# Idle matmuls ahead of 57 chosen items of TensorE, and a newly searched order of all queues, in a fused recurrence, attention and mixture-of-experts kernel

## The chip, the cores and the metric

One Trainium2 chip, one of its cores. The time is that of one execution on the device in microseconds, from its start to its end, as the median of several runs. TensorE multiplies, VectorE (DVE) and ScalarE (ACT) do the elementwise work, GpSimd (POOL) does the additions of the recurrence and some masks, and SyncE (SP) issues every DMA, one after the other in one written order.

## The reference

The input x has the shape (4, 1024, 256). Two layers follow one another, each as x + layernorm(layer(layernorm(x))).

```python
# layer 1: a gated recurrence over the 1024 steps of time
px = x @ W_state.T + b_state
g  = sigmoid(x @ W_gate.T + b_gate)
state = tanh(px[t] + state); out[t] = g[t] * state
# layer 2: attention, then a mixture of four experts
q, k = rms(heads(h @ wq.T)), rms(heads(h @ wk.T)); v = heads(h @ wv.T)     # 16 heads of 16
x = x + softmax(causal(q @ k.T / 4)) @ v @ wo.T                            # first 64 columns set to 0
w = top 2 of 4 of softmax(xf @ gate_w.T), renormalised
o0 = gelu(xf @ e0_up.T) @ e0_down.T
o1 = silu(xf @ e1_w1.T) * (xf @ e1_w2.T) @ e1_down.T
o2 = gelu(gelu(gelu(xf @ e2_l1.T) @ e2_l2.T) @ e2_l3.T) @ e2_l4.T
o3 = gelu(gelu(xf @ e3_down.T) @ e3_up.T) @ e3_out.T
x = x + sum_e w[e] * o_e                                                   # first 64 columns set to 0
```

## The kernel before, in words

The work is cut into items. An item is a key such as `("qk", 3, 0)` and stands for a handful of instructions of one engine, or for one transfer of SP. There are 1648 items of TensorE, 909 transfers, 1100 items of DVE, 840 of ACT and 98 of POOL, and beside these the 1024 steps of the recurrence, each a pair of `sadd` (POOL, L1959) and `stanh` (ACT, L1185).

First comes a stage of 8 tiles of 128 moments of time for all four batches: load x (`xin`), layernorm on DVE (`hst`, `hsc`), transpose on TensorE (`htr`), copy (`hcp`), the two products with W_state and W_gate (`hpx0`, `hpx1`), and the store of what is needed later (`hsv`). It ends with `hpx0, 7`. Beside it and after it 19 pieces of the expert weights are loaded (`wl`), split by DVE into a rounded part that stays and a remainder (`wsh`, `wsp`, L1593 and L1599), and the remainders are written back to memory (`wst`, L1041). The load of a piece waits for the split of the fourth one before it, since they share four buffers.

Then come 16 units u of 256 rows (`NU`), each one a chain: load of the gate values (`gl`), gating with the state of the recurrence on DVE (`pgate`), transposes (`ptr`), load of x (`xl`), two layernorms on DVE (`pln`, `pu`), `qh`, `qtr`, the products for q, k and v (`qk`, `vm`), their normalisation on DVE (`qrs`, `kh`, `qq`), transposes (`kt`, `qt`), tiles of scores for the row maxima (`mxm` on TensorE, `mxr` on DVE), `mtr`, `mta`, a small transfer `mtd`, then scores, exponentials and weighted values (`sc`, `ex`, `av`), the output projection (`wo`), the router (`gm`, `ga`, `gb`), and the experts: `up`, `gel`, `dn` with weights that SP loads anew for each unit (`wr`). The last step of a unit is `fin` and its store `ost`. Units overlap: the experts of one unit run beside the attention of the next ones.

What sets the order. `Plan.sequence` merges all items into one list. `PLACES` gives, kind by kind, the place of each item in that list, and `STEPS` tells how many items stand between a step of the recurrence and the next. Each engine executes its items in this order, with nothing reordered at run time, and each item first waits on the semaphores of what it needs. `Plan.run` goes once through the list with estimated durations, and from that decides which of the eight banks of PSUM and which buffer each item gets; a bank or buffer that was held before adds a wait (`turn`, `freed`). `ISSUE`, `RATE` and `FLIGHT` are its estimates for transfers. The estimated times are used for nothing else.

On TensorE an item waits first for its bank (`freed(key, "P2")`, `freed(key, "P1")`), then for its operands. `mm` at L1299 is a matmul, `tr` at L1302 a transpose, L1383 the transposes of `kt` and `qt`. A plain f32 product stands in the profile as two matmul records, one of rounded operands or a transpose as one. The pool `MB` (two buffers, taken by `mxm`, given back by `mxr`) exists in the plan; the code of `mxm` waits for its bank, but not for `MB`.

Of the kernel before, what the change touches and what calls it, by code (L numbers as in the profile page):

```python
# [42 lines left out]
BANKS = {"P2": 2, "P1": 1}  # L43
# [3 lines left out]
HOP = 0.04  # L47
# [4 lines left out]
ISSUE, RATE, FLIGHT = 0.47, 300.0, 1.7  # L52
# [4 lines left out]
    "wl": (9, 6, 10, 4, 5, 8, 53, 209, 99, 227, 222, 229, 3, 198, 208, 206, 199, 221, 223, 219, 214, 256, 242, 255, 226,  # L57
        267, 250, 286, 282, 291, 264, 290),
    "cbx": (24,),
    "cqk": (237,),  # L60
    "wsp": (101, 132, 98, 129, 211, 218, 216, 213, 240, 236, 241, 225, 263, 245, 279, 244, 284, 262, 289, 378, 303, 327,
        329),
    "wsh": (210, 217, 215, 212, 234, 233, 239, 224, 261, 243, 278, 235, 281, 259, 288, 283, 297, 280, 302),
    "wst": (220, 231, 228, 309, 252, 266, 257, 232, 319, 268, 354, 477, 287, 265, 320, 471, 475, 433, 470),
    "wdd": (308, 598, 137, 269),
    "xin": (0, 7, 26, 54, 55, 96, 102, 150),
    "hst": (11, 21, 28, 69, 71, 118, 128, 179),
    "hsc": (13, 16, 12, 14, 25, 37, 41, 22, 39, 40, 38, 42, 75, 73, 70, 76, 74, 77, 78, 72, 121, 120, 123, 119, 134, 130,
        131, 133, 182, 181, 183, 180),
    "htr": (15, 17, 18, 19, 43, 45, 46, 47, 44, 48, 50, 51, 81, 82, 83, 84, 85, 86, 87, 88, 124, 125, 126, 135, 140, 141,  # L70
        142, 143, 185, 186, 189, 190),
    "hcp": (20, 49, 52, 89, 110, 144, 147, 191),
# [3 lines left out]
    "hgt": (30, 31, 32, 33, 34, 35, 36, 64, 65, 66, 67, 91, 92, 93, 59, 60, 62, 68, 106, 107, 108, 104, 105, 109, 112, 113,  # L76
        114, 115, 136, 152, 153, 155, 157, 161, 163, 159, 160, 162, 165, 166, 170, 171, 156, 167, 168, 169, 172, 173, 174,
        193, 195, 196, 201, 202, 203, 204),
    "hout1": (61, 94, 116, 117, 164, 176, 175, 205),
    "hsv": (95, 97, 138, 139, 149, 178, 151, 194, 187, 188, 207, 230),  # L80
    "ident": (1,),
    "consts": (2,),
    "pxl": (530, 1523),
    "gl": (100, 251, 478, 352, 805, 960, 1026, 1141, 1557, 1748, 1809, 1910, 2710, 2271, 2970, 3072),
    "xl": (247, 258, 536, 473, 954, 968, 1074, 1219, 1750, 1802, 1872, 2242, 2942, 2415, 3020, 3427),
    "pgate": (238, 253, 497, 452, 930, 964, 1043, 1184, 1702, 1781, 1828, 1934, 2737, 2323, 3010, 3195),
    "ptr": (246, 254, 506, 459, 933, 966, 1049, 1207, 1716, 1787, 1830, 2218, 2934, 2396, 3016, 3409),
    "pcp": (248, 271, 580, 487, 940, 972, 1062, 1209, 1722, 1793, 1836, 2239, 2952, 2406, 3032, 3412),
    "pln": (249, 272, 589, 488, 963, 1000, 1081, 1247, 1752, 1819, 1876, 2286, 2979, 2416, 3034, 3439),
# [3 lines left out]
    "qtr": (273, 307, 614, 511, 985, 1016, 1109, 1293, 1769, 1859, 2130, 2332, 3013, 2528, 3125, 3498),  # L93
    "qhT": (274, 312, 617, 513, 992, 1024, 1114, 1303, 1772, 1863, 2132, 2335, 3023, 2548, 3170, 3501),
    "qhl": (275, 314, 618, 518, 994, 1047, 1126, 1322, 1783, 1940, 2139, 2351, 3028, 2552, 3174, 3508),
    "qk": (276, 292, 317, 331, 621, 635, 522, 541, 995, 1006, 1050, 1085, 1201, 1225, 1326, 1381, 1815, 1831, 1987, 2020,
        2148, 2211, 2370, 2472, 3033, 3080, 2614, 2756, 3307, 3338, 3521, 3694),
    "qkc": (277, 294, 326, 333, 622, 638, 523, 543, 999, 1010, 1057, 1088, 1208, 1230, 1332, 1386, 1818, 1837, 2012, 2021,
        2158, 2220, 2374, 2477, 3035, 3083, 2617, 2766, 3314, 3342, 3526, 3697),
    "qred": (285, 295, 330, 335, 630, 656, 529, 556, 1003, 1012, 1065, 1091, 1214, 1248, 1365, 1393, 1826, 1841, 2013, 2057,  # L100
# [3 lines left out]
    "vst": (310, 392, 778, 566, 1078, 1143, 1370, 1530, 1873, 2243, 2315, 2720, 3208, 2909, 3509, 3855),  # L104
    "qrs": (296, 336, 659, 557, 1015, 1093, 1253, 1394, 1850, 2058, 2232, 2483, 3093, 2783, 3359, 3722),
# [6 lines left out]
    "kst": (311, 321, 355, 393, 674, 693, 569, 647, 1048, 1098, 1190, 1223, 1278, 1313, 1428, 1518, 1875, 1911, 2080, 2118,  # L112
# [7 lines left out]
    "ktm": (322, 323, 324, 353, 405, 406, 430, 431, 705, 706, 735, 736, 804, 821, 859, 860, 1102, 1104, 1107, 1142, 1224,  # L120
# [4 lines left out]
    "mxm": (339, 340, 344, 345, 359, 360, 363, 364, 367, 369, 370, 373, 375, 376, 383, 384, 409, 410, 414, 416, 422, 423,  # L125
# [259 lines left out]
)  # L385


class Plan:

# [1606 lines left out]
```

## Time and profile before

| | us |
|---|---|
| median of 3 runs | 1581.17 |
| lowest, highest | 1580.75, 1584.56 |
| the profiled execution | 1590.62 |
| its span, first to last instruction | 1588.9 |
| TensorE busy in it | 1401.2 (88%) |
| mean granted TensorE clock | 0.933 |

The profile is of one execution. Busy times are the time in which an engine had an instruction in it. The granted clock is 1.0 where TensorE was allowed its full 2.4 GHz and 0.5 where it got 1.2 GHz; the page shows it in 40 slices, and a stretch of the trace can be asked for its mean. An idle time in square brackets is the engine's own just before the row, with what ended it.

### The profile page before, as it was taken

What the parts mean: (1) busy time and instruction counts of PE and PEld (TensorE: products, weight loads), DVE (VectorE), ACT (ScalarE), POOL (GpSimd) and SP (SyncE); (2) the same over time, 40 slices, a digit from 0 to 9 for tenths busy, and PEclk for the clock granted to TensorE, in tenths of its full rate; (3) what the DMA queues carried; (4) which work ended last, traced back from release to release, by engine and by line L of the source; (5) the groups of instructions that cost most, each with busy time, mean ns of one, the idle gap of its engine ahead of it and who ended that gap; (6) DMA issues with size and microseconds to landing.
All of it is one profiled execution on the core that took longest, in us unless ns stands there. A gap on an engine that the chain in (4) does not pass through costs nothing.

```text
span 1588.9 us, 33612 instructions
## 1 busy us (share of the span) xinstructions
PE 1401.2 (88%) x12320; PEld 1111.7 (70%) x12320; DVE 1098.1 (69%) x2916; ACT 884.0 (56%) x2042; POOL 310.1 (20%) x1146
## 2 busy tenths in 40 slices
PE   6924679888999799997999999999999899999997
PEld 3413568877788468875878668875788557885797
DVE  6856466655688876668888777778799648783334
ACT  2544546654665585576555773437631686337942
POOL 3333223332233332223233110001000010001000
PEclk9966569997999799998999999998999999999999
DMA  3464455674467457664547646585667566676544
GB/s 113 141 212 146 138 173 151 181 205 144 149 181 220 142 145 215 192 187 128 194 144 219 201 139 199 149 247 155 185 187 228 154 215 192 200 221 189 158 144 134
DMA packets 244275, 278.53 MB, mean 175 GB/s; under 512 B 37136, under 2 KB 167696, under 8 KB 243856
## 3 DMA queue, kind: packets, MB, share of 16 engines
q1 hardware_dynamic: 244112, 276.39, 58.0%
q8 instruction: 99, 1.62, 0.4%
q14 instruction: 64, 0.52, 0.1%
HBM read 234.18 MB, written 43.45 MB: 175 GB/s over the span
## 4 chain that ended last, share of the span: by engine, by line
PE 59%; DMA 12%; DVE 10%; ACT 9%; issue 5%; SPq 3%; POOL 3%; ACTq 0%; DVEq 0%
PE PS L1299 54%; DMA KT<-ktd 5%; ACT work L1253 3%; PE PS L1302 3%; POOL AD L1959 2%; DMA WB<-wlo_e_l 2%; ACT PX L1185 2%; PE PS L1383 1%; DVE mx L1758 1%; DMA WB<-wdn_e_down 1%; DVE st L1576 1%; DMA work<-in_L_ffn_e_l 1%; DMA UU<-in_L_attn_x 1%; POOL work L1966 1%; SPq L1051 1%
## 5 line engine op out<-in xcount | busy, mean ns | idle before, releaser
L1185 ACT ACTIVATE PX<-AD 128x8 f32<-128x8 f32 x1023 | 219.7, 215 | 253.8 <-POOL AD L1959 252.6
L1959 POOL TENSOR_TENSOR AD<-PX 128x8 f32<-128x8 f32 x1023 | 242.4, 237 | 580.4 <-ACT PX L1185 567.5
L1253 ACT ACTIVATE work<-PS 128x1024 f32<-128x1024 f32 (+1 forms) x312 | 286.2, 959 | 77.7 <-PE PS L1299 76.7
L1758 DVE TENSOR_REDUCE mx<-PS 128x2 f32<-128x1024 f32 (+3 forms) x256 | 256.7, 1020 | 64.8 <-PE PS L1299 64.3
L1299 PE MATMUL PS<-work,vlx 128*32 128x256 f32 (+2 forms) x2816 | 242.5, 388 | 19.0 <-ACT work L1253 5.4
L1278 ACT ACTIVATE work<-PS 128x512 f32<-128x512 f32 x176 | 102.5, 593 | 177.4 <-PE PS L1299 176.7
L1299 PE MATMUL PS<-EP,u_e_l 128*128 128x256 f32 x1024 | 195.0, 285 | 7.0 <-DMA WB<-wlo_e_l 4.8
L1299 PE MATMUL PS<-WB,work 128*128 128x192 f32 x1024 | 186.4, 337 | 7.5 <-DMA WB<-wdn_e_down 4.7
L1966 POOL TENSOR_SCALAR_AFFINE_SELECT work<-work 128x512 f32<-128x512 f32 x96 | 63.0, 667 | 625.5 <-ACT work L1253 625.4
L1299 PEld LDWEIGHTS PS<-WB,work 128*128 128x128 f32 x1024 | 170.7, 195 | 12.8 <-issue 6.2
L1299 PE MATMUL PS<-EP,WB 128*128 128x256 f32 x640 | 179.3, 280 | 0.0
L1299 PEld LDWEIGHTS PS<-EP,u_e_l 128*128 128x128 f32 x1024 | 161.1, 189 | 10.6 <-issue 4.9
L1299 PEld LDWEIGHTS PS<-work,vlx 128*32 128x32 f32 (+1 forms) x2816 | 90.6, 118 | 109.9 <-issue 52.2
L1299 PE MATMUL PS<-KT,QT 64*128 64x512 f32 (+3 forms) x768 | 146.6, 427 | 22.4 <-DMA KT<-ktd 9.9
L1299 PE MATMUL PS<-XF,WB 128*128 128x256 f32 x576 | 163.9, 285 | 0.0
L1299 PE MATMUL PS<-QT,KT 64*128 64x256 f32 (+1 forms) x1344 | 143.9, 320 | 20.5 <-DMA KT<-ktd 7.9
L1299 PEld LDWEIGHTS PS<-QT,KT 64*128 64x128 f32 x1344 | 102.1, 199 | 83.4 <-issue 57.3
L1758 DVE TENSOR_REDUCE mxb<-PS 128x2 f32<-128x256 f32 (+3 forms) x128 | 104.8, 819 | 31.2 <-PE PS L1299 30.7
L1299 PEld LDWEIGHTS PS<-EP,WB 128*128 128x128 f32 x640 | 121.2, 189 | 0.1
L1299 PEld LDWEIGHTS PS<-KT,QT 64*128 64x128 f32 x768 | 72.0, 197 | 62.8 <-issue 29.9
L1299 PEld LDWEIGHTS PS<-XF,WB 128*128 128x128 f32 x576 | 111.5, 194 | 0.1
L1299 PE MATMUL PS<-XF,u_e_w 128*128 128x256 f32 x512 | 101.6, 287 | 1.7 <-DMA WB<-wlo_e_w 1.7
(170 smaller groups left out, 2244.8 us busy)
## 6 DMA issues: line engine op xcount, KB each, us to landing
KT<-ktd SPq DMA_DIRECT2D x112, 512.0 KB, 5.0
WB<-wlo_e_l SPq DMA_DIRECT2D x160, 256.0 KB, 4.1
ktd<-KTs SPq DMA_DIRECT2D x128, 128.0 KB, 2.6
WB<-wlo_e_up SPq DMA_DIRECT2D x64, 256.0 KB, 3.5
WB<-wlo_e_w SPq DMA_DIRECT2D x64, 256.0 KB, 3.7
WB<-wdn_e_down SPq DMA_DIRECT2D x64, 192.0 KB, 3.0
KT<-ktd SPq DMA_DIRECT2D x48, 256.0 KB, 3.7
KT<-ktd SPq DMA_DIRECT2D x32, 384.0 KB, 4.2
```

The lines of the kernel that those rows point to most:

```text
L1051: eng.dma_start(plain(WB[place[key, "W"]][:, :, 0:src.shape[2]]), src).then_inc(of(*key), 16)
L1185: eng.activation(cur, AD[n % 2], ACT.Tanh).then_inc(of(*key), 1)
L1253: eng.activation(pt[:, :, :, q0:L], two("sc", *a).rearrange("p a (l q) -> p a l q", l=2)[:, :, :, q0:L], ACT.Exp).then_inc(of(*key), 1)
L1278: eng.activation(half_of(hidden(u, name), h), one("up", u, name, h), ACT.Gelu).then_inc(of(*key), 1)
L1299: return eng.matmul(o, l, r, start=start, stop=stop, skip_group_check=skip)
L1302: return eng.transpose(o, i, ident)
L1383: ins = eng.transpose(ps[:, p // 4, 128 * (p % 4):128 * (p % 4) + 128].bitcast(F32R), QKP[:, 2 * p:2 * p + 2, :].rearrange("p h r -> p (h ...
L1576: step(eng.bn_stats(s_[:, i, :], src[:, i, :]))
L1758: eng.tensor_reduce(o, two("mxm", *a)[:, :, 0:w], AX, ALU.max, negate=True).then_inc(of(*key), 1)
L1959: eng.tensor_tensor(AD[n % 2], PX[c % 2][:, :, :, t], PX[(n - 1) // L % 2][:, :, :, (n - 1) % L], ALU.add).then_inc(of(*key), 1)
L1966: eng.affine_select(out=p, in_=p, compare_op=ALU.is_ge, fill=0.0, base=0, pattern=[[0, 2], [0, 2], [1, 128]], channel_multiplier=-1).then_ ...
```

## The change

Three things are changed.

- A table `WARM` names 57 items of TensorE and a number for each, 190 in all. Ahead of such an item, after the wait for its bank and before the wait for its operands, TensorE does that many f32 products of the identity with itself, 128 x 128 by 128 columns, into the bank that the item holds and is about to overwrite. Their results are used by nobody.
- `PLACES` and `STEPS` are new tables throughout. Of the 1648 items of TensorE 709 change their place in TensorE's own order, 136 of them by three places or more and 8 by ten or more (at most 16). Of SP's 909 transfers 766 move, 370 by three or more and 85 by ten or more (at most 83). Of DVE's 1100 items 755 move, 203 by three or more. Of ACT's 840 items 405 move, 74 by three or more. On POOL 4 items move by one.
- The estimates of the plan are changed: issue and flight times by kind of transfer in place of 0.47 and 1.7 for all, and the idle products are in its account of TensorE's time and of its clock. They act on the kernel through the choice of banks and buffers alone.

The core of the diff, without the number tables:

```diff
-ISSUE, RATE, FLIGHT = 0.47, 300.0, 1.7
+RATE, IDLE = 300.0, 0.222
+ISSUE = {"kst": 0.66, "vst": 0.54, "mtd": 0.73, "gl": 0.64, "kts": 0.62, "vl": 0.62, "wr": 0.6, "x1l": 0.62}
+FLIGHT = {"gl": 2.55, "hsv": 1.55, "kst": 0.55, "ktm": 2.35, "kts": 2.55, "ost": 2.05, "vl": 2.25, "vst": 3.55, "wr": 2.1, "wl": 2.25,
+          "wst": 1.65, "x1l": 2.25, "x1st": 1.95, "xin": 1.95, "xl": 1.75, "pxl": 3.5, "wdd": 2.15, "mtd": 1.35}
...
+WARM = {
+    ("aot", 0): 1, ("aot", 2): 1, ("av", 0, 3, 0): 4, ("av", 1, 0, 0): 6, ("av", 1, 1, 0): 1, ("av", 10, 1, 0): 3,
+        ("av", 2, 1, 0): 2, ("av", 6, 3, 0): 1, ("dn", 11, "e2_l4"): 5, ("dn", 15, "e3_out"): 4, ("dn", 2, "e1_down"): 7,
+        ("dn", 6, "e3_out"): 3, ("gm", 2): 9, ("gm", 7): 1, ("hpx0", 0): 3, ("kt", 0, 0): 7, ("kt", 0, 1): 2,
+        ("kt", 1, 0): 5, ("kt", 4, 0): 3, ("kt", 6, 0): 6, ("mtr", 3): 4, ("mxm", 0, 2): 11, ("mxm", 0, 6): 6,
+        ("mxm", 1, 10): 2, ("mxm", 1, 13): 1, ("mxm", 1, 5): 1, ("mxm", 13, 23): 2, ("mxm", 2, 10): 2, ("mxm", 3, 9): 5,
+        ("mxm", 5, 1): 3, ("mxm", 5, 11): 1, ("mxm", 5, 4): 3, ("ptr", 0): 7, ("ptr", 1): 8, ("ptr", 4): 1, ("qk", 0, 0): 8,
+        ("qk", 0, 1): 2, ("qk", 1, 0): 2, ("qk", 15, 0): 1, ("qk", 8, 1): 4, ("qt", 2, 0): 3, ("qt", 8, 0): 2,
+        ("qtr", 0): 2, ("qtr", 2): 2, ("qtr", 3): 1, ("qtr", 5): 1, ("sc", 0, 1, 0): 1, ("sc", 1, 0, 0): 1,
+        ("sc", 1, 2, 0): 12, ("sc", 12, 0, 0): 1, ("sc", 9, 3, 0): 1, ("up", 0, "e0_up", 0): 4, ("up", 15, "e2_l2", 0): 2,
+        ("up", 8, "e2_l3", 0): 1, ("vm", 2): 1, ("wo", 0): 2, ("wo", 1): 5
+}
...
+                if key in WARM:
+                    bank = PS[:, place[key, "P2" if (key, "P2") in place else "P1"], :]
+                    pe.wait_ge(*done("ident"))
+                    for _ in range(WARM[key]):
+                        mm(bank[:, 0:128], ident, ident, True, True, True)
```

In `Plan.run` the idle products are run from the moment at which the bank is free in the plan, `IDLE` us each at the full clock and twice that at half of it, and the item starts after them. The plan's account of the clock counts its stretches from the start of the plan, before and after the change.

In SP's order the transfers that the prediction speaks of stand as follows. Before, `hsv, 7, 1` (the last store of gate values) stood at place 45 of SP's list, behind thirteen loads of weights (`wl`), among them `e2_l2, 1, 1`, and behind two stores of remainders (`wst`). Now it stands at place 42, behind the loads of `e1_w2` and `e2_l1` and behind `wst, e0_up, 0, 0`, and ahead of all loads of `e2_l2`, of `wl, n1` and of `wst, e1_w1, 0, 0`. `wl, qn`, which stood just ahead of it, is at place 29. `wl, wo` has gone from place 34 to place 101. Between `xl, 0` and `gl, 1` stood one load; now a store and a load stand there.

## Rows read from the trace of the kernel before

**Rows 1.** The page: busy time of each engine; TensorE and clock by slices; the chain.

```profile
PE 1401.2 (88%) x12320; PEld 1111.7 (70%) x12320; DVE 1098.1 (69%) x2916; ACT 884.0 (56%) x2042; POOL 310.1 (20%) x1146
...
PEclk9966569997999799998999999998999999999999
...
PE 59%; DMA 12%; DVE 10%; ACT 9%; issue 5%; SPq 3%; POOL 3%; ACTq 0%; DVEq 0%
```

**Rows 2.** Busy time by stages: stretch, length, each engine, granted clock, DMA share, GB/s.

```profile
85.00:160.00 75.00, 22.34 (x95) 16.60 (x94) 49.01 (x139) 31.16 (x127) 27.09 (x105) 0.64 0.61 186
160.00:230.00 70.00, 49.95 (x462) 38.01 (x460) 37.18 (x119) 32.23 (x103) 17.49 (x78) 0.59 0.54 162
...
230.00:1588.90 1358.90, 1261.77 (x11580) 1024.89 (x11580) 952.02 (x2469) 784.11 (x1655) 236.46 (x836) 0.96 0.60 179
```

**Rows 3.** The same view, of the seventeen half-clock stretches between 230 and 1580 us.

```profile
417.22:424.05 6.83, 6.83 (x73) 4.96 (x72) 5.86 (x23) 5.24 (x9) 0.61 (x3) 0.50 0.37 115
...
sum 92.17, PE 84.58 PEld 66.05 DVE 62.82 ACT 43.88 POOL 21.62; mean PE 4.98 PEld 3.89 DVE 3.70 ACT 2.58 POOL 1.27
```

**Rows 4.** The same view, of the half-clock stretches between 90 and 230 us.

```profile
164.64:209.01 44.37, 35.48 (x351) 27.98 (x352) 23.05 (x61) 18.46 (x62) 12.01 (x52) 0.50 0.48 137
...
sum 112.63, PE 59.25 PEld 45.53 DVE 69.89 ACT 47.11 POOL 32.96; mean PE 14.81 PEld 11.38 DVE 17.47 ACT 11.78 POOL 8.24
```

**Rows 5.** TensorE's timeline, 85 to 170 us: start, length, instruction, [idle before <- what ended it].

```profile
106.22 1.09 PE L1302 MATMUL PS<-ident,G 128*128 128x128 f32 x4 [18.56 <-DMA gd<-work]
...
114.88 1.12 PE L1302 MATMUL PS<-ident,G 128*128 128x128 f32 x4 [7.57 <-DVE G L1674]
...
126.16 1.19 PE L1299 MATMUL PS<-wqkv,hT 128*128 128x512 f32 x2 [3.85 <-DVE hT L1615]
...
140.49 1.23 PE L1383 MATMUL PS<-identr,QKP 128*128 128x128 f32 x8 [7.87 <-DVE QKP L1749]
...
168.63 1.23 PE L1383 MATMUL PS<-identr,QKP 128*128 128x128 f32 x8 [2.06 <-DVE QKP L1749]
```

**Rows 6.** SP's timeline around the last store of gate values.

```profile
94.33 0.47 SPq L1041 DMA_DIRECT2D wlo_e_up<-WB  x1
...
99.50 0.52 SPq L1062 DMA_DIRECT2D gd<-work  x1
```

**Rows 7.** TensorE's timeline: two rows at half clock, two at full clock.

```profile
227.35 1.11 PE L1302 MATMUL PS<-ident,G 128*128 128x128 f32 x4
228.25 1.06 PE L1302 MATMUL PS<-ident,HA 128*128 128x128 f32 x4
...
610.98 2.87 PE L1299 MATMUL PS<-WB,work 128*128 128x192 f32 x16
613.68 0.60 PE L1302 MATMUL PS<-ident,HA 128*128 128x128 f32 x4
```

**Rows 8.** TensorE's waits after 230 us: for whom, us in total, times, longest.

```profile
PE PS L1299 <- DMA KT<-ktd: 14.1, 14, 3.4
PE PS L1299 <- ACT work L1253: 12.2, 20, 1.9
...
PE PS L1299 <- DMA WB<-wlo_e_l: 5.8, 5, 2.9
```

**Rows 9.** TensorE's timeline: first and last of 34 `WARM` items after 230 us.

```profile
230.19 0.63 PE L1302 MATMUL PS<-ident,HA 128*128 128x128 f32 x4 [0.87 <-DVE HA L1718]
...
1578.37 1.86 PE L1299 MATMUL PS<-WB,work 128*128 128x192 f32 x10 [0.78 <-ACT work L1278]
```

**Rows 10.** TensorE's timeline: the longest wait for a transfer after 160 us.

```profile
224.31 1.12 PE L1299 MATMUL PS<-QT,KT 64*128 64x128 f32 x8 [3.65 <-DMA KT<-ktd]
```

**Rows 11.** DVE's gating of unit 4, and two steps of the recurrence on ACT behind it.

```profile
402.17 0.69 DVE L1670 SCALAR_TENSOR_TENSOR G<-G,PX 128x512 f32<-128x512 f32 x1 [0.50 <-ACT PX L1185]
...
403.48 0.21 ACT L1185 ACTIVATE PX<-AD 128x8 f32<-128x8 f32 x1 [0.31 <-POOL AD L1959]
404.01 0.22 ACT L1185 ACTIVATE PX<-AD 128x8 f32<-128x8 f32 x1 [0.31 <-POOL AD L1959]
```

More of the change, by code:

```diff
@@ L56 @@
 PLACES = {
[L57 to L64, printed above, removed]
@@ new lines @@
+    "cbx": (27,),
+    "cqk": (228,),
+    "wsp": (227, 135, 75, 102, 210, 204, 207, 209, 236, 229, 250, 237, 262, 239, 285, 280, 278, 261, 296, 356, 338, 312,
+        409),
+    "wsh": (208, 203, 205, 206, 233, 226, 232, 225, 252, 235, 282, 277, 276, 260, 295, 326, 284, 279, 357),
+    "wst": (223, 266, 238, 242, 473, 258, 289, 246, 263, 257, 406, 471, 351, 286, 403, 394, 431, 321, 434),
+    "wdd": (319, 255, 106, 7),
+    "xin": (0, 4, 24, 54, 57, 100, 108, 150),
+    "hst": (8, 18, 44, 55, 69, 103, 130, 167),
@@ L125 @@
-    "mxm": (339, 340, 344, 345, 359, 360, 363, 364, 367, 369, 370, 373, 375, 376, 383, 384, 409, 410, 414, 416, 422, 423,
[19 rows of a table removed]
-    "mxr": (341, 342, 348, 347, 361, 362, 365, 366, 368, 371, 372, 374, 379, 377, 387, 386, 413, 412, 418, 419, 424, 425,
[19 rows of a table removed]
-    "mtr": (388, 463, 769, 893, 1216, 1351, 1588, 1717, 2128, 2371, 2772, 2995, 3387, 3575, 3982, 4181),
-    "mta": (389, 467, 771, 894, 1217, 1363, 1607, 1762, 2129, 2372, 2782, 3012, 3396, 3597, 3984, 4191),
-    "mtd": (396, 476, 781, 911, 1222, 1368, 1649, 1805, 2133, 2402, 2794, 3021, 3426, 3598, 4038, 4253),
[4 rows of a table removed]
@@ new lines @@
+    "gl": (194, 245, 474, 265, 584, 954, 1031, 1163, 1591, 1759, 1807, 1879, 2821, 2240, 2973, 3216),
+    "xl": (241, 259, 535, 493, 952, 997, 1042, 1218, 1707, 1806, 1877, 2268, 2971, 2414, 3017, 3411),
+    "pgate": (230, 251, 483, 455, 932, 963, 1032, 1171, 1693, 1766, 1844, 1992, 2866, 2301, 3008, 3221),
+    "ptr": (231, 254, 505, 468, 933, 979, 1033, 1196, 1697, 1783, 1856, 2222, 2940, 2397, 3012, 3409),
+    "pcp": (240, 269, 528, 491, 936, 983, 1034, 1202, 1698, 1811, 1858, 2230, 2957, 2400, 3026, 3431),
@@ new lines @@
+    "pln": (243, 270, 587, 499, 955, 999, 1078, 1226, 1736, 1813, 1883, 2287, 2978, 2440, 3031, 3440),
[3 rows of a table added]
+    "qtr": (271, 303, 613, 511, 981, 1015, 1115, 1283, 1770, 1870, 2114, 2326, 3011, 2519, 3124, 3496),
+    "qhT": (272, 310, 616, 513, 982, 1025, 1116, 1292, 1779, 1889, 2125, 2337, 3020, 2540, 3160, 3505),
+    "qhl": (273, 311, 621, 519, 991, 1052, 1124, 1319, 1782, 1937, 2131, 2338, 3025, 2557, 3167, 3509),
+    "qk": (274, 291, 315, 329, 624, 632, 522, 541, 993, 1007, 1059, 1084, 1199, 1215, 1322, 1380, 1791, 1827, 1981, 2019,
+        2152, 2215, 2369, 2472, 3029, 3079, 2609, 2758, 3307, 3338, 3520, 3695),
@@ new lines @@
+    "kst": (305, 318, 354, 391, 671, 704, 592, 642, 1049, 1094, 1181, 1222, 1277, 1359, 1426, 1524, 1882, 1911, 2079, 2120,
[7 rows of a table added]
+    "ktm": (322, 323, 350, 353, 404, 405, 432, 433, 707, 730, 739, 740, 788, 828, 860, 861, 1099, 1100, 1161, 1180, 1223,
[4 rows of a table added]
+    "mxm": (336, 337, 343, 344, 358, 360, 362, 364, 366, 367, 369, 375, 377, 379, 381, 382, 411, 413, 414, 416, 422, 423,
[19 rows of a table added]
+    "mxr": (339, 340, 348, 347, 359, 361, 363, 365, 368, 370, 371, 376, 378, 380, 384, 383, 412, 415, 419, 421, 425, 426,
[19 rows of a table added]
+    "mtr": (385, 476, 784, 898, 1211, 1347, 1580, 1721, 2129, 2383, 2769, 2993, 3388, 3575, 3991, 4176),
@@ L431, in run, with clock, stream, enter @@
         got, end, busy, mode, wire = {}, {}, dict.fromkeys(self.order, 0.0), dict.fromkeys(self.order), 0.0
-        streamed, window, slow = defaultdict(float), 0, False
+        streamed, window, slow, after = defaultdict(float), 0, False, None
+        def clock(t):
+            nonlocal window, slow
+            while (window + 1) * WINDOW <= t:
+                slow = t > FRESH and streamed[window] / WINDOW < (HIGH if slow else LOW)
+                window += 1
+            return 2.0 if slow else 1.0
+        def stream(t, us):
+            t1 = t + us
+            while t < t1:
+                w = int(t / WINDOW + 1e-9)
+                streamed[w] += min(t1, (w + 1) * WINDOW) - t
+                t = min(t1, (w + 1) * WINDOW)
+        def enter(m, gap):
+            if m != mode["pe"]:
+                mode["pe"] = m
+                return ENTER[m] + max(0.0, (LEAVE.get(after, 0.095) if after else 0.0) - gap)
+            return ENTER[m] if gap > 0.05 else 0.0
         for k in self.sequence():
             e, us, take, m, kb = self.items[k]
-            t = max([busy[e]] + [end[a] if (a, k) in self.queue else self.over[a] + HOP for a in self.after[k]])
+            bank, t = 0.0, max([busy[e]] + [end[a] if (a, k) in self.queue else self.over[a] + HOP for a in self.after[k]])
             for p in take:
@@ L454, in run @@
                 t = max(t, a)
+                if p in BANKS:
+                    bank = a
                 self.place[k, p] = got[k, p][0]
@@ L461, in run @@
             if e == "pe":
-                while (window + 1) * WINDOW <= t:
-                    slow = t > FRESH and streamed[window] / WINDOW < (HIGH if slow else LOW)
-                    window += 1
-                us *= 2.0 if slow else 1.0
-                t0, t1 = t, t + us
-                while t0 < t1:
-                    w = int(t0 / WINDOW + 1e-9)
-                    streamed[w] += min(t1, (w + 1) * WINDOW) - t0
-                    t0 = min(t1, (w + 1) * WINDOW)
-                gap = t - busy[e]
-                if m != mode[e]:
-                    us += ENTER[m] + max(0.0, (LEAVE.get(self.order[e][-1][0], 0.095) if self.order[e] else 0.0) - gap)
-                elif gap > 0.05:
-                    us += ENTER[m]
-                mode[e] = m
+                if k in WARM:
+                    t1 = max(busy[e], bank)
+                    for i in range(WARM[k]):
+                        d = IDLE * clock(t1)
+                        if i == 0:
+                            d += enter("128", t1 - busy[e])
+                        stream(t1, d)
+                        t1 += d
+                    busy[e], after = t1, "idle"
+                    t = max(t, t1)
+                us *= clock(t)
+                stream(t, us)
+                us += enter(m, t - busy[e])
+                after = k[0]
             elif m and m != mode[e]:
@@ L482, in run @@
                 wire = max(wire, t + us) + kb / RATE
-                over = wire + FLIGHT
+                over = wire + FLIGHT[k[0]]
             self.order[e].append(k)
@@ L542, in dma @@
     def dma(key, kb, *after, n=1, **more):
-        add("sp", key, ISSUE * n, *after, kb=float(kb), **more)
+        add("sp", key, ISSUE.get(key[0], 0.52) * n, *after, kb=float(kb), **more)
     for i, w in enumerate(("x0", "bs", "bg", "x1", "q", "k", "v", "wo", "gw", "n1", "n2", "qn", "kn")):
```

120 lines of the change are left out of this document (54 added, 66 removed), and 490 rows, old and new, of tables (PLACES, STEPS).

## The prediction

> **What bounds the kernel now.** I read the page first. TensorE is busy 1401.2 of 1588.9 us, no other engine more than 1098.1, and the chain that ended last is TensorE for 59% [rows 1]. The slices of the clock add what the busy time hides: a dip to 0.5 and 0.6 early on, and single slices of 0.7 later [rows 1]. Then I cut the span into stages. From 230 us on TensorE is busy 1261.77 of 1358.90 us, so it is the bound there and only 97 us are idle; from 85 to 160 us it is busy 22 of 75 us, from 160 to 230 us 50 of 70 us [rows 2]. The second stretch is bound by a chain: the loads and splits of the weights, and unit 0 going from engine to engine.
>
> Last I asked for the stretches at half clock, 1.2 in place of 2.4 GHz. Between 230 and 1580 us there are seventeen, 92.17 us long with TensorE busy 84.58 of them [rows 3]. Work that takes 84.6 us at half clock takes some 42 us at full clock: 42 us is all that the clock has to give there. Between 90 and 230 us there are four, 112.63 us with 59.25 us busy; in the longest of them, 164.64 to 209.01 us, it is 35.48 of 44.37 us [rows 4]. In the other three TensorE mostly waits, and a faster clock shortens only what the chain passes through.
>
> **The price of an idle product.** A plain product of 192 columns at full clock takes (613.68 - 610.98) / 16 = 0.169 us a record, which for two records of 128 columns makes 2 x 0.169 x 128/192 = 0.225 us. At half clock four records of 128 columns take 228.25 - 227.35 = 0.90 us, so a product of two records takes 0.45 us [rows 7]. The 190 products are 43 us of TensorE at full clock and 86 at half. Whether they cost anything depends on the wait that they stand in. I laid the places of `WARM` on the trace of before. 95 products lie before 230 us and 95 behind it.
>
> **Part 1, SP's order at 85 to 110 us.** The first transposes of unit 0 wait 18.56 us, until 106 us, for the store of gate values [rows 5]. That store is issued at 99.50 us [rows 6]: ahead of it stand loads and stores that wait for DVE's splits. In the new order it stands right behind `wst, e0_up, 0, 0`, which before was issued at 94.33 us [rows 6], and the loads of `e2_l2` that block are behind it. That is 99.5 - 95.0 = 4.5 us. The next step of unit 0, `xl`, is issued behind `ptr`, and the transposes of unit 1, at 114.88 us [rows 5], depend on `gl, 1`, which is moved along. Bounds: 0, if the gating on DVE or the landing is late instead, and 8. I take **-4.5**. Moved past the store are the loads of `e2_l2`, which now come later; what hides this is that their weights are first used after 250 us.
>
> **Part 2, the clock up to 160 us.** Ahead of `ptr`, `ptr`, `qtr`, `qk` and `kt` of units 0 and 1 stand 7, 8, 2, 8 and 7 products, at most 3.6 us at half clock; four of the five waits they stand in are 18.56, 7.57, 3.85 and 7.87 us long [rows 5]. They are free. They come at the start of the wait, so of a long wait most stays idle, and I don't expect the level to hold through 8 or 18 us. Where the wait is as long as the products (`qk, 0, 0`: 8 x 0.45 = 3.6 of 3.85 us) the level can be up for what follows. The chain passes through `qk` and `kt` for about 4 us at half clock; half of it is **-2**, bounds 0 and -4.
>
> **Part 3, 160 to 230 us.** `mxm, 0, 2` gets 11 products, `kt, 1, 0` five and `mxm, 0, 6` six. Before, `mxm, 0, 2` followed its predecessor without a gap; the plan sees a wait there for `MB`, which the code doesn't have. The next real wait is the 2.06 us at `kt, 1, 0` [rows 5]. The 22 products take 5 us at full clock and 10 at half, less 2.06: 3 to 8 us late, beside DVE's work on the keys in part; queued behind them are the tiles of scores that DVE reduces, and behind these `mtr` and the transfer of the maxima. I take +3. If the clock is up for the 35.48 busy us [rows 4], that gives up to 17.7; ACT's exponentials and DVE pace part of it, so I take -8. The 18 products at `sc, 1, 2, 0` and `av, 1, 0, 0` are 4.1 us at full clock beside the 3.65 us for the transfer of keys that stands two items on [rows 10]: nothing. Together **-5**, bounds +8 and -15.
>
> **Part 4, the clock after 230 us.** Of the seventeen stretches twelve have items of `WARM` in them or in the 8 us ahead, with 61.6 of the 84.58 busy us; five, such as 417.22 to 424.05 us, have none [rows 3]. The twelve could give 30.8 us. The level falls after thin stretches, and the order of hundreds of items around has changed, so new dips will come; I take half, -15. The 95 products cost 21.4 us. Of the 34 items 18 stood behind a gap of 0.15 us or more, the first 0.87 us, the last 0.78 us [rows 9]; gap by gap these cover 9.8 us. Of the other 11.6 us I take half as cost, +6, since the new order can have put a wait where the trace has none. Together **-9**, bounds +12 (no clock) and -25.
>
> **Part 5, the order after 230 us.** The waits for keys and for the experts' remainders sum to 19.9 us [rows 8]. Better issue and flight times place loads earlier, -3. A TensorE that is faster in places runs into ACT and POOL; there are 12.2 us of waits for the exponentials already [rows 8]: +3. Together **0**, bounds -12 and +10.
>
> **The sum.** -4.5 - 2 - 5 - 9 + 0 = -20.5 us. The profiled execution took 1590.62 us, 9.4 more than the median of 1581.17; as the terms are differences, I set them against the median: 1581.2 - 20.5 = **1560.7 us**.
>
> **The rivals.**
> Products without their clock. They were placed for a clock that the plan counts from its own start. If the level in a run changes at other moments, the dips stay and the products remain. The trace speaks for it in part: the five stretches without any product nearby show that the plan didn't expect them. Price: parts 2 and the -8 and -15 fall away, the products cost 3 + 6 and up to the full 3 + 11.6, against -4.5: +4.5 to +10, so about 1588 us, slower. It decides where less than 9 us of the clock's gain come. [...] Chance 0.11. The Trainium skill ("TensorE: Matmul & The Clock Gate", Part 1) says that the gate's count runs free and isn't reset at a kernel's start, so that the same kernel meets it at a different phase each time; no single trace can show that, and by it this rival is the natural one.
>
> The gain goes into other waits. TensorE is relieved, and DVE, ACT and transfers are late next. At unit 4 there is a place for this: its gating ran right behind the 512th step of the recurrence, at 402.17 us [rows 11], 4 us ahead of its transposes, so that a lead of more than that before 400 us is lost unless the recurrence comes earlier too. For that speaks that undisturbed steps follow at 0.53 us (404.01 - 403.48, [rows 11]), while 512 steps by 402 us are 0.79 each: they are held up by ACT's other work, which would move along. If half of parts 3 and 4 is lost this way: -4.5 - 2 - 7 = 1568 us, between 1564 and 1577. Chance 0.22.
>
> Nothing is left. Part 1 is hidden by DVE, and clock and products cancel: 1580 us. Chance 0.09.
>
> All of it holds. The twelve stretches give 25 us and the long one at 165 us gives 12: 1541 us. Chance 0.08.
>
> **How the numbers follow.** The forecast, 1550 to 1573 us, has 0.50. Within 0.3%, about what a measurement of this kernel can tell from no change, is 1576.4 to 1585.9. Faster: 0.50 + 0.08 + 0.20 of the 0.22 = 0.78; same: 0.09 + 0.02 = 0.11; slower 0.11. For 8 in 10 the range reaches from 1544 to 1582.
>
> **What would show it.** Part 1: the store of gate values issued at about 95 us and the first transposes of unit 0 at 101 to 102 us. Part 2: `qk, 0, 1` at full clock. Part 3: `kt, 1, 0` late by 1 to 5 us, and the scores of unit 0 nevertheless 3 to 9 us earlier, with the clock at 1.0 up to 209 us. Part 4: half-clock stretches after 230 us of 50 to 60 us in place of 92, and a mean clock of 0.95 or more. Part 5: TensorE's waits for keys and remainders not above 20 us. I am wrong if the half-clock time after 230 us is above 80 us, if TensorE's other waits grow by more than 10 us, or if unit 0 starts no earlier.

## The result, and the profile after

The changed kernel takes 1536.83 us (1536.3 to 1538.04, 4 runs) against 1582.87 us (1580.75 to 1584.91, 4 runs): ratio 0.9696, 95% interval 0.9666 to 0.9726. That is 46 us faster. I had forecast 20 us and a range down to 1544 us. The sign was right, the size was not. The two profiled executions lie 54 us apart (1590.62 and 1536.93 us): that of the kernel before was 8 us above its median, so differences between the two traces are too large by about that much.

The page of the changed kernel: busy times, TensorE's clock in 40 slices, the chain that ended last.

```profile
span 1535.2 us, 34359 instructions
...
PE 1417.4 (92%) x12700; PEld 1138.7 (74%) x12700; DVE 1096.4 (71%) x2916; ACT 877.5 (57%) x2038; POOL 311.9 (20%) x1146
...
PEclk9977689999999899999999999999999999999999
...
PE 69%; DVE 12%; ACT 7%; DMA 4%; issue 4%; POOL 2%; SPq 2%; ACTq 0%; DVEq 0%
```

Beside [rows 1] TensorE is busy 16 us longer and the span is 54 us shorter. The 380 new matmul records are the 190 products. The main change is in the chain: transfers held 12% of it, now 4%. The late slices of 0.7 are gone from the clock; the early dip is shorter, but it is there.

The same stages as in [rows 2], cut where unit 0 has come as far (224 us), and the sum of the half-clock stretches after that, for [rows 3]:

```profile
85.00:156.00 71.00, 32.84 (x174) 29.23 (x173) 48.58 (x139) 33.49 (x130) 26.73 (x98) 0.71 0.64 195
156.00:224.00 68.00, 58.08 (x562) 47.60 (x562) 36.77 (x112) 27.48 (x94) 16.50 (x76) 0.72 0.52 151
224.00:1535.20 1311.20, 1258.24 (x11774) 1027.90 (x11771) 951.88 (x2477) 780.05 (x1656) 239.84 (x839) 0.99 0.62 186
...
sum 30.71, PE 29.18 PEld 19.69 DVE 19.79 ACT 15.40 POOL 7.44; mean PE 4.17 PEld 2.81 DVE 2.83 ACT 2.20 POOL 1.06
```

The gain lies in the third stage. Its length went from 1358.9 to 1311.2 us, its idle time from 97 to 53 us, though 95 products fill part of it, and its half-clock time from 92.2 us in seventeen stretches to 30.7 in seven.

TensorE's longest waits there, for [rows 8]:

```profile
PE PS L1337 <- ACT work L1291: 7.4, 19, 1.4
PE PS L1337 <- POOL work L2009: 5.5, 9, 1.5
PE PS L1426 <- DVE QKP L1792: 4.7, 6, 1.4
PE PS L1337 <- DVE mx L1801: 3.7, 9, 0.9
PE PS L1337 <- DMA KT<-ktd: 3.1, 2, 2.0
```

The waits for keys were 14.1 us and are 3.1. The waits for the experts' remainders `wlo_e_l`, 5.8 us, and for `wdn_e_down` are no longer among them; the latter stood in the kernel before as

```profile
PE PS L1299 <- DMA WB<-wdn_e_down: 4.7, 4, 2.2
```

The waits for ACT's exponentials became shorter too, not longer: 12.2 us before, 7.4 now.

Where the lead arises can be read by laying the items of the two traces on one another. The last expert product of a unit comes earlier by 6 us in unit 1, 22 in unit 3, 34 in unit 5, 54 in unit 8, and by 54 in unit 15: it grows from 350 to 1010 us and not at all afterwards.

### The profile page after: what moved, and what is told of

Its sections match the earlier page's. It is cut to its first block, busy times and chain, and to the rows that moved or that the text cites. A ratio compares the mean times of both kernels' runs of the same rounds, so it can differ in the third digit from the quotient of the medians.

```text
span 1535.2 us, 34359 instructions
## 1 busy us (share of the span) xinstructions
PE 1417.4 (92%) x12700; PEld 1138.7 (74%) x12700; DVE 1096.4 (71%) x2916; ACT 877.5 (57%) x2038; POOL 311.9 (20%) x1146
## 4 chain that ended last, share of the span: by engine, by line
PE 69%; DVE 12%; ACT 7%; DMA 4%; issue 4%; POOL 2%; SPq 2%; ACTq 0%; DVEq 0%
PE PS L1337 64%; PE PS L1340 3%; ACT work L1291 3%; PE PS L1426 2%; POOL AD L2002 1%; DVE mx L1801 1%; ACT PX L1223 1%; DMA KT<-ktd 1%; DMA vlx<-vd 1%; DVE st L1619 1%; DMA WB<-wlo_e_w 1%; DVE mxb L1801 1%; POOL work L2009 1%; ACT work L1316 1%; DVE rst L1606 0%
## 5 line engine op out<-in xcount | busy, mean ns | idle before, releaser
L1337 PE MATMUL PS<-work,vlx 128*32 128x256 f32 (+2 forms) x2816 | 236.2, 378 | 14.6 <-POOL work L2009 5.5
L1337 PE MATMUL PS<-WB,work 128*128 128x192 f32 x1024 | 182.2, 332 | 1.0 <-ACT work L1316 0.6
L1337 PEld LDWEIGHTS PS<-WB,work 128*128 128x128 f32 x1024 | 166.5, 191 | 5.2 <-issue 1.8
L1337 PE MATMUL PS<-XF,WB 128*128 128x256 f32 x576 | 160.8, 279 | 0.0
L1337 PE MATMUL PS<-KT,QT 64*128 64x512 f32 (+3 forms) x768 | 144.0, 419 | 10.5 <-DVE mx L1801 4.3
L1337 PEld LDWEIGHTS PS<-QT,KT 64*128 64x128 f32 x1344 | 97.2, 191 | 69.2 <-issue 47.4
L1337 PE MATMUL PS<-QT,KT 64*128 64x256 f32 (+1 forms) x1344 | 137.3, 311 | 8.8 <-DMA KT<-ktd 3.1
L1337 PEld LDWEIGHTS PS<-XF,WB 128*128 128x128 f32 x576 | 108.3, 188 | 0.2
```

The lines of the kernel that those rows point to most:

```text
L1337: return eng.matmul(o, l, r, start=start, stop=stop, skip_group_check=skip)
```

## The experiments

For each trace I give four numbers of one stretch, from the transposes of unit 0 in its expert part (`xtr, 0`) to the last expert product: its length, TensorE's idle time in it, how much of that idle time a transfer ended, and the excess of the clock, which is half of TensorE's busy time in half-clock stretches. They come from single executions, and executions of one kernel scatter: 64 runs of the kernel before, on four chips, took 1574.0 to 1595.0 us. The times and ratios come from all runs of a kernel; a ratio is to the kernel before on the same chip, whose median was 1582.9 to 1586.9 us.

| kernel | median us | ratio to before (95%) | length | idle | by transfers | half-clock us (stretches) | excess |
|---|---|---|---|---|---|---|---|
| before | 1582.9 | | 1350.1 | 90.1 | 31.1 | 93.4 (18) | 42.8 |
| changed | 1536.8 | 0.9696 (0.9666-0.9726) | 1300.7 | 45.3 | 7.8 | 30.7 (7) | 14.6 |
| changed, again (e9) | 1539.5 | 0.9700 (0.9666-0.9734) | 1298.0 | 44.0 | 6.9 | 27.3 (5) | 12.2 |
| new order, no products (e1) | 1540.8 | 0.9699 (0.9665-0.9733) | 1309.0 | 66.5 | 14.3 | 57.4 (9) | 24.7 |
| the same again (e10) | 1543.5 | 0.9711 (0.9676-0.9746) | 1310.7 | 65.8 | 11.4 | 61.0 (10) | 26.7 |
| old order, products (e2) | 1592.6 | 1.0029 (1.0000-1.0058) | 1346.1 | 76.1 | 19.7 | 58.0 (13) | 27.1 |
| changed, late products only (e3) | 1540.9 | 0.9707 (0.9677-0.9738) | 1303.3 | 46.1 | 10.8 | 37.0 (7) | 16.8 |
| transposes for products (e4) | 1537.1 | 0.9692 (0.9648-0.9736) | 1298.9 | 48.2 | 10.5 | 23.9 (4) | 9.8 |
| SP's order old, rest new (e5) | 1623.3 | 1.0238 (1.0174-1.0303) | 1363.7 | 96.1 | 35.6 | 109.8 (20) | 48.2 |
| SP's order new, rest old (e6) | 1672.7 | 1.0557 (1.0493-1.0621) | 1407.7 | 117.2 | 31.2 | 161.4 (24) | 71.8 |
| old order, new banks (e7) | 1596.8 | 1.0081 (1.0046-1.0115) | 1359.8 | 90.6 | 24.2 | 106.7 (18) | 48.1 |
| TensorE's order old, rest new (e8) | 1732.2 | 1.0933 (1.0871-1.0996) | 1485.5 | 169.8 | 22.6 | 209.5 (38) | 90.9 |
| fitted products (e11) | 1535.5 | 0.9668 (0.9635-0.9701) | 1296.8 | 36.1 | 3.0 | 17.1 (3) | 7.9 |
| first part new (e12) | 1571.7 | 0.9891 (0.9854-0.9928) | 1337.7 | 84.0 | 22.7 | 75.4 (13) | 32.9 |
| second part new (e13) | 1573.6 | 0.9934 (0.9911-0.9957) | 1341.4 | 85.0 | 21.1 | 85.3 (12) | 37.6 |
| old order, 14 transfers ahead (e14) | 1580.6 | 0.9971 (0.9951-0.9991) | 1335.8 | 80.7 | 15.5 | 81.9 (13) | 36.8 |
| old order, one store ahead (e15) | 1586.8 | 1.0019 (0.9998-1.0040) | 1346.0 | 95.2 | 29.5 | 73.3 (12) | 30.5 |

### Order or products?

Run e1 leaves the products out of the changed kernel, e2 puts them into the one before.

```diff
-                if key in WARM:
+                if key in ():
```

> The changed kernel with its new order and its choice of banks and buffers, but without the 190 idle products on TensorE. Theory A (the new order gives the larger part, because TensorE waits less for transfers; the products give the rest through the clock): 1548 to 1558 us, half-clock time after 230 us between 55 and 90 us, TensorE's waits for transfers after 230 us at most 15 us, as in the changed kernel. Theory B (the products give nearly all of it through the clock): 1570 us or more. Theory C (the products do nothing that the order would not do alone): 1535 to 1540 us.

> The kernel before, in its old order, with the same 190 products ahead of the same 57 items. Theory A: between 1568 and 1585 us: the clock gives back 10 to 20 us and the products that stand in no wait cost 5 to 15; the waits for transfers stay at about 30 us. Theory B: 1545 to 1560 us. The rival of the prediction (products without their clock): 1585 to 1592 us.

The new order alone gives 45 us (0.9699). The products alone, in the old order, give nothing and rather cost 5 us (1.0029). For the time of e1 theory C was nearest (1535 to 1540 us), and A, with an order worth 28 to 38 us, was 7 us off; A's two other marks held (57.4 us at half clock, 14.3 us of waits for transfers). For e2 no theory held: by the time the rival, 1585 to 1592 us, was nearest.

The order's gain adds up in the table: idle time 90.1 to 66.5 (-23.6), clock 42.8 to 24.7 (-18.1), together -41.7 of a length that fell by 41.1. So the order, which says nothing of clocks, gave back about as much of the clock as the products: 18.1 us here and 16.1 in the second trace of this kernel (e10), against 15.7 for the products in the old order (e2) and 10.1 and 14.5 in the new one. TensorE's waits in the order-only kernel, e1, after unit 0:

```profile
PE PS L1337 <- ACT work L1291: 8.1, 16, 1.2
PE PS L1426 <- DVE QKP L1792: 8.0, 8, 1.4
PE PS L1337 <- DVE mx L1801: 6.0, 12, 1.2
...
PE PS L1337 <- DMA WB<-wdn_e_down: 3.5, 2, 2.0
...
PE PS L1337 <- DMA KT<-ktd: 2.9, 5, 0.9
```

The keys and most of the remainders have left the list here already, with no product in the kernel.

In e2 the products do give back clock, 42.8 to 27.1, and fill waits, 90.1 to 76.1; that is 29.7 us. But 95 products take at least 21.4 us, the stretch is only 4.0 us shorter in all, and before it unit 0 comes 5.8 us later (234.1 in place of 228.3 us). In all: nothing.

The ten runs of e2 show something that one trace can't: how much clock comes back differs from run to run, and the time with it. The mean granted clock was 0.946 in the slowest (1600.2 us) and 0.964 in the fastest (1580.8 us). Each of the ten is above all 64 runs of the kernel before, 0.925 to 0.941.

### The products, within the new order

> The changed kernel itself once more, to stand beside the order-only kernel on the same chip. 1535 to 1542 us.

> The order-only kernel (changed kernel without its 190 products) once more, on the same chip as the changed one. The two medians of different calls were 4 us apart. If the products are worth something in the new order: 3 to 6 us above the changed kernel. If they are worth nothing: within 2 us.

On one chip the changed kernel took 1539.5 us (1530.5 to 1546.8) and the order-only one 1543.5 us (1533.3 to 1546.9). That is 4 us, as between e1 and the first result, but the runs overlap widely; the products are worth about 4 us, and these runs don't rule out that they are worth nothing. What they do to the clock is beyond doubt: its mean is 0.956 to 0.965 in the ten runs with products (the first four and e9) and 0.940 to 0.949 in the ten without (e1 and e10). The traces show how: from e10 to e9 the clock gives 14.5 us, the idle time falls by 21.8, and the products take 21.4; the stretch is 12.7 us shorter, in the other pair 8.3. The profiled run of e9 was its fastest and that of e10 nearly its slowest, so 12.7 is too much. The dips that stay are mostly at the same places: the changed kernel's at 507.5, 524.5, 558.7 and 698.6 us are found in e9, some 6 us ahead, at 500.9, 518.0, 552.1 and 692.0 us.

Run e3 has the late products only:

```diff
-                if key in WARM:
+                if key in WARM and key not in EARLY:
```

> The changed kernel with only the 95 products of the 34 items after 230 us; the 95 ahead of the 23 items before that are left out. Since unit 1 came only 2 to 4 us earlier at 224 us in the changed kernel, theory A expects the early products to be worth 0 to 4 us: 1536 to 1541 us. If the 22 products that stand in no real wait in the first tiles of scores cost time (my step 3 of the prediction), it is below 1535 us. If the early clock is worth what I took (10 us), 1545 us or more.

1540.9 us, ratio 0.9707. It can't be told from the changed kernel, nor from the order-only one. The 95 early products are worth at most a few us either way.

### Do transposes hold the clock up as well?

```diff
-                    for _ in range(WARM[key]):
-                        mm(bank[:, 0:128], ident, ident, True, True, True)
+                    for _ in range(2 * WARM[key]):
+                        tr(bank[:, 0:128], ident)
```

> The changed kernel with each idle product replaced by two transposes of the identity into the same bank, which occupy TensorE for the same time (0.11 us each at full clock). If transposes hold the clock up as products do, it is the same as the changed kernel, 1535 to 1540 us, with 30 to 40 us at half clock after 230 us. If they don't count for the clock, it is near the order-only kernel plus what the transposes cost where they stand in no wait: 1555 to 1570 us, with 60 us or more at half clock after 230 us.

They do: 1537.1 us, and 23.9 us at half clock after unit 0 against 57 and 61 us without products and 27 to 31 with them. The mean granted clock of the four runs is 0.953 to 0.962, that of the ten runs without products at most 0.949. The Trainium skill ("TensorE: Matmul & The Clock Gate", Part 4) says that transposes don't count for the clock as other work does; by that this kernel should have had about as much half-clock time as without products, 57 to 61 us. This case's trace doesn't agree, for f32 transposes of the identity; the duration that the page gives is of bf16 ones.

### Whose order?

For e5, e6 and e8 each engine keeps the order of one of the two kernels, and the plan merges the five lists anew, taking from each only what can run. Where nothing can, it takes an item ahead of its turn: 11 times in e5, 53 in e6, 35 in e8. Banks and buffers are chosen anew each time.

```diff
-        for k in self.sequence():
+        rnk = {k: (prev if v[0] in FROM_OLD else new)[k] for k, v in self.items.items()}
+        queues = {e: sorted((k for k in self.items if self.items[k][0] == e), key=rnk.get) for e in self.order}
...
+        for k in following():
```

> No idle products. The new order for TensorE, ACT, DVE and POOL; the transfers of SP as near as can be to the order of the kernel before (11 times an item had to be taken ahead because nothing else could run). Order-only kernel: 1541 us; before: 1586 us. Theory S (the gain sits in SP's order: transfers issued in time): 1565 to 1590 us, TensorE's waits for transfers after unit 0 at 25 us or more as before (31.1), against 14.3 in the order-only kernel. Theory E (it sits in the order of the engines): 1540 to 1555 us with 15 to 20 us of such waits.

> No idle products. The reverse: TensorE, ACT, DVE and POOL in the order of the kernel before, SP's transfers in the new order (53 forced exceptions). Theory S: 1545 to 1565 us. Theory E: 1575 us or more. A third theory, T (the orders fit only together): slower than the kernel before, over 1590 us, here and in the run with the old order of SP.

> No idle products. Only TensorE in the order of the kernel before, all else new (35 forced exceptions). Theory S: 1545 to 1560 us, since TensorE's order isn't what mattered. If TensorE's own order carries the gain: 1570 us or more.

> No idle products. All engines and SP in the order of the kernel before (one forced exception), but banks and buffers chosen with the new estimates of transfer times: 1468 of the choices differ from the kernel before. If the choice of banks and buffers carries part of the gain: 1565 us or less. If not (my expectation): 1580 to 1592 us.

All three mixtures are slower than the old kernel, by 2.4, 5.6 and 9.3%, though both parents are faster: theory T. In e5 more than half of that is lost before the stretch of the table: unit 0 is at 249.95 us in place of 228.25. TensorE's order, of which 136 items move by three or more places, makes a kernel of 1732 us when it is the old one amid new neighbours, 148 us above the kernel before and 191 above the order-only one. The page's clock line of e8 shows the damage:

```profile
PEclk9966568997989889989898999999999899999999
```

So the gain can't be ascribed to one queue. How much of the loss is due to the mixed orders, and how much to the items taken ahead and to other banks and buffers (in each mixture over 40% of these choices differ from its parent's), these runs don't separate; e7, with one such item and 1468 of 3487 choices changed, is 0.8% slower than before. So in the old order the choice by the new estimates gives nothing; in the new order it wasn't tried by itself.

### Where in time, and do late transfers explain it?

```diff
+        cut = prev[('dn', 4, 'e3_out')]
+        rnk = {k: new[k] if prev[k] <= cut else 99999 + prev[k] for k in self.items}
```

> No products. All queues in the new order up to the last expert product of unit 4, in the order of the kernel before from there on; an item goes with the half in which the old order has it (no forced exceptions). If the gain of the order is a sum of many local ones: about 28 of 45 us, as the lead at that point is, so 1552 to 1562 us. If the orders of early and late parts depend on one another: above 1575 us.

> No products. The complement of e12: all queues in the order of the kernel before up to the last expert product of unit 4, in the new order from there on (3 forced exceptions). If the gain of the order is a sum of local ones, e12 (-15 us) and this one together give what the order-only kernel gives (-43 to -45 us), so 1555 to 1562 us. If it needs the whole: 1575 us or more.

The first part new gives 15 us (by ratio 17), the second part new 10; together 25 to 28 of 45. The traces show where the rest went: e12 leads by 28.5 us at the last expert product of unit 4, as the order-only kernel does (27.8), and by 19.3 two units later. The old order that follows gives back 9 us. Behind the cut the order-only kernel gains another 20 us and e13 10. Neither run met an expectation: both lie between the two, nearer the one by which early and late parts depend on one another. Some 25 to 28 us of the gain are there with one part alone; the other 17 to 20 need both.

For e14 I looked up, for each of the old kernel's waits for a transfer, when its buffer had come free and when SP issued it. Fourteen had been issued late, thirteen by 1 to 7 us and one by 98 us: they stood behind other transfers. (The one of 98 us, `vl, 2, 1`, was moved ahead by three places, which is 5 of them.) The longest wait is that of `mxm, 5, 8`, 3.45 us: its keys' buffer was free at 536.2 us, SP was busy with the four parts of the store `kst, 6, 0` until 539.7, and the keys landed 5.2 us after issue, at 545.0. SP's timeline of the kernel before:

```profile
537.18 2.54 SPq L1107 DMA_DIRECT2D ktd<-KTs  x4
539.76 0.62 SPq L1120 DMA_DIRECT2D KT<-ktd  x1
```

```diff
+        for key, ahead_of in MOVED:
+            self.order["sp"].remove(key)
+            self.order["sp"].insert(self.order["sp"].index(ahead_of), key)
```

> The kernel before, with 14 transfers of keys, values and weights moved ahead by one to three places in SP's list, to where their buffer had come free in the trace; TensorE waited 15.5 us in all for these. Nothing else is changed, no products. If late transfers are what the new order cured: 10 to 25 us faster than before (15 us of waits, and the half-clock stretches that follow them), and waits for transfers after unit 0 at 15 us in place of 31. If they only went along: within 5 us of the kernel before.

1580.6 us against 1584.0, ratio 0.9971 (0.9951 to 0.9991): 5 us by the ratio. The waits for transfers did fall by half, 31.1 to 15.5, as far as in the order-only kernel (14.3); the gain didn't follow (the profiled run of e14, 1574.88 us, was one of its fastest, so that the stretch in the table looks better than the median). This is TensorE's list of waits in e14:

```profile
PE PS L1319 <- ACT work L1273: 16.5, 24, 1.9
PE PS L1403 <- DVE QKP L1769: 7.9, 8, 2.8
PE PS L1319 <- DMA KT<-ktd: 6.0, 8, 1.3
...
PE PS L1319 <- DMA WB<-wlo_e_l: 4.9, 3, 3.2
```

The waits for ACT's exponentials rose from 12.2 to 16.5 us. TensorE came sooner and stood before other engines. The new order removes both kinds at once (e1: 8.1 and 14.3), and these fourteen moves don't. Late transfers are a cause: these fourteen give about a tenth of the gain in the old order. What carries the rest stays open. That it is spread over hundreds of places, in which the five lists are shifted to one another, fits the runs but isn't shown by them.

### The one step at the start

```diff
+    (('hsv', 7, 1), ('wl', ('e1_w2', 0, 0))),
```

> The kernel before, with one transfer moved: the last store of gate values, from behind seven loads and stores to right behind the store of the first remainder, as in the new order. My step 1: the first transposes of unit 0 start 4 us earlier, at 102 us. In the changed kernel the lead of 4 us at that point was 4 us at 224 us as well. If it lives on: 3 to 5 us faster than before. If the order further on is built around the later start and gives it back: within 2 us.

The store was issued at 98.37 us, only 1.1 us earlier than in [rows 6], and unit 0's first transposes came 1.7 us later, at 107.91, in place of 4 us earlier. Two views of e15 tell why. ACT's timeline (start, length, operation, idle time before it):

```profile
96.96 1.38 ACT L1202 ACTIVATE work<-PS,bx 128x128 f32<-128x128 f32 x5
```

The same row in the kernel before:

```profile
95.76 1.38 ACT L1195 ACTIVATE work<-PS,bx 128x128 f32<-128x128 f32 x5
```

DVE's timeline of e15:

```profile
105.24 0.76 DVE L1600 CAST u_e_w<-work 128x512 fp32r<-128x512 f32 x2 [7.02 <-DMA work<-in_L_ffn_e_w]
...
107.05 0.75 DVE L1681 SCALAR_TENSOR_TENSOR G<-G,PX 128x256 f32<-128x256 f32 x2
```

The store waits for ACT's last sigmoid piece, which ends at 96.96 + 1.38 = 98.3 us; in the kernel before it ends at 95.76 + 1.38 = 97.1. SP was never 4.5 us late, but 2.4 (99.5 - 97.1). Also, e15 isn't the move of the new order, though its expectation says so: it puts the store ahead of the two loads of `e1_w2`, which the new order leaves ahead of the store. Moved so, SP stands at the store, the loads behind it start late, DVE waits 7.02 us for them, and the gating of unit 0 stands behind DVE's splits. The changed kernel does have its first transposes at 102.48 us, near the forecast of 101 to 102, but by other means. Its timeline of ACT:

```profile
94.83 1.38 ACT L1233 ACTIVATE work<-PS,bx 128x128 f32<-128x128 f32 x5
```

And that of SP's queue:

```profile
96.79 0.52 SPq L1100 DMA_DIRECT2D gd<-work  x1
```

ACT ends at 96.2 and the store follows at 96.79 us, with enough loads ahead of it.

### Products fitted to measured waits

> The new order with another set of products: 161 of them at 41 items, all after 200 us, each number fitted to a wait for operands (not for a bank) that the trace of the order-only kernel shows there, so many as fill that wait at 0.225 us each. If products in measured waits cost nothing and hold the clock up: 1526 to 1536 us, below the changed kernel, with half-clock time after unit 0 at 0 to 20 us. If the clock isn't what is left to gain: 1535 to 1541 us.

1535.5 us (1529.9 to 1542.2), ratio 0.9668 (0.9635 to 0.9701), against 1539.5 and 0.9700 of the changed kernel on the same chip. That lies in both ranges that I had written down, so the time doesn't decide between them. After unit 0 two places are left at half clock, 504.4 to 524.9 us in two stretches and 1026.7 to 1030.1 us, about 17 us in all, where the changed kernel has 27 to 31. It is the fastest median of all, but 4 us within such a spread is no proof that it beats the changed kernel. It does show that after unit 0 little is left in the clock: its excess there is 7.9 us.

## Why the prediction was wrong, point by point

**What bounds the kernel.** Right: TensorE from 230 us on, and the gain lies there. That 42 us was all that the clock had to give there holds too: 28 of it came back.

**The price of a product.** Right. At full clock ten records took 1.14 us (from 164.23 to 165.37 us of the changed kernel), 0.228 us a product; I had 0.225.

```profile
164.23 1.38 PE L1337 MATMUL PS<-ident 128*128 128x128 f32 x10
165.37 0.88 PE L1426 MATMUL PS<-identr,QKP 128*128 128x128 f32 x8
```

**Part 1, SP's order at the start, -4.5.** The number came out in one trace (first transposes 3.7 us earlier), the reason didn't. In the other traces with the new order from the start they come 1.0 to 3.1 us earlier (e1, e3, e4, e9 to e12), and in e7, with SP's old order, 2.4 us, so that even these can't be put down to SP's order. I read the queue ahead of the store and not what the store itself waited for. That is one more question to the same trace: where does its releaser end? Run e15 shows that moving the store by itself is no gain: it was issued 1.1 us earlier, the transposes came 1.7 us later, and the kernel took 1.0019 (0.9998 to 1.0040) of the time.

**Parts 2 and 3, clock and products up to 230 us, -7.** Not borne out. `qk, 0, 0` and the second half of it do run at full clock now, as foreseen:

```profile
122.27 1.64 PE L1337 MATMUL PS<-wqkv,hT 128*128 128x512 f32 x6 [0.51 <-DVE hT L1658]
123.75 0.61 PE L1337 MATMUL PS<-ident 128*128 128x128 f32 x4
124.11 1.65 PE L1337 MATMUL PS<-wqkv,hT 128*128 128x512 f32 x6
```

But `xtr, 0` comes at 223.9 and 220.2 us with the products and at 221.2 and 223.6 without: no difference. And the long stretch at half clock is still there, 172.96 to 207.09 us (in e9 in two pieces, 173.2 to 186.9 and 197.1 to 203.9 us). The 11 products ahead of `mxm, 0, 2` took 4.2 us, from 159.53 to 163.69 us. I had called the wait there one that the code doesn't have; the order-only kernel, e1, shows a real one of 1.9 us, for a bank that DVE's reduction of the maxima gives back, so about half of their cost was covered:

```profile
161.55 0.47 PE L1337 MATMUL PS<-KT,QT 64*128 64x128 f32 x2 [1.92 <-DVE mx L1801]
```

In the old order the early products cost the 5.8 us that I had feared (bounds +8).

**Part 4, the products' clock after 230 us, -9.** Right in size within the new order: the stretch is 8.3 and 12.7 us shorter with them, by 10.1 and 14.5 us of clock, for which I had -15. By the medians the products are worth about 4 us. In the old order the stretch was 4 us shorter with them. Half-clock time after 230 us came out at 31 us, where I had named 50 to 60: the order alone had brought it to 57 and 61.

**Part 5, the new order, 0: this is the step that failed.** It measured -41 in the stretch of the traces (-39 in e10), a few us of which may be the slow profiled execution of the kernel before; by the medians the order-only kernel is 45 and 43 us faster in all. I had put -3 for transfers and +3 given back to ACT. Three things were wrong in it. The waits for transfers fell by 17 us and not by 3. I had read 19.9 us of them, keys and `wlo_e_l` alone, where all together were 31; and the reason for the 3, better estimates, was none, since the estimates act only through banks and buffers, and e7 has no gain from them; only SP's new list could place a load earlier. The waits for ACT fell too, from 16.8 to 10.6 us in the stretch, though I had them grow (those for DVE grew, from 28.8 to 32.2). And I had counted a wait at its own length. In the table, idle time and excess go together: from the order-only kernel to e8 103 us more idle come with 66 us more excess, 0.64 for each; from before to order-only it is 18.1 for 23.6, 0.77; a straight line through the eleven kernels without products has 0.66. So, on average over these kernels, a microsecond of waiting goes with about 1.7 us of time. That is no law for a single one: e15 has 5 us more idle than the kernel before and 12 less excess. I had given the whole of the clock to the products, and the order has about half of it.

**The rivals.** "Products without their clock", slower by 4 to 10 us, is what happened in the old order (e2, +5 us), but by its price, not its mechanism: some of the clock did come back in each run, and the products ate it. By the rule of the Trainium skill named there ("TensorE: Matmul & The Clock Gate", Part 1), that the gate's count runs free, the gain should vary from run to run. The runs agree as far as that: the changed kernel's first four lie within 1.8 us of one another, but e9, the same kernel, ranges over 16 us, with the granted clock at 0.965 in the fastest and 0.956 in the slowest run, and e2 over 19. That the phase is the reason no run here shows. "The gain goes into other waits" is seen in e14. The recurrence didn't hold anything up: its 512th step ended at 391.8 us, 10 us earlier, so it moved along as I had argued. "All of it holds", 1541 us at 0.08, was the nearest number, with the wrong items in its sum.

## What to carry to other kernels

When a change reorders every queue, don't set its effect to zero because no single move can be argued: take TensorE's idle time by releaser, all of it, as the stake, and price a us of it at more than one, by the clock's excess that the trace shows per idle us. Filling waits with idle work is worth little where the waits can be removed, and costs its full length where no wait is. Before calling a transfer late because of its queue, look up when its own releaser ended; and judge an order as a whole, since a good queue amid another's neighbours was slower than the poor one. And read more than one execution: the granted clock differs between runs of one kernel.

## What the runs showed of the hardware

Transposes of the identity kept the clock at its full level as well as products of the same duration did (23.9 us at half clock after unit 0, against 27 to 31; mean clock 0.953 to 0.962, against 0.956 to 0.965). The granted clock differed from run to run of one kernel on one chip, and the time with it: in e2 0.946 at 1600.2 us and 0.964 at 1580.8. Where TensorE waited for a transfer after 224 us of the kernel before, it had landed 2.4 to 7.1 us after its issue, with a median of 5.2, while the profile's medians by kind are 2.6 to 5.0 us for transfers of 128 to 512 KB. And a static order is brittle: with TensorE's old list amid the new lists of the others, 35 forced exceptions and other banks and buffers, a kernel of 1541 us took 1732 us.
